# One-hot comparisons for an edge-count matrix: buckets of 512 targets instead of 256, made by two per-part comparisons instead of one interleaved one

## The chip, the cores and the metric

One core of one Trainium2 chip. The metric is device microseconds of one execution of the whole kernel, median of three runs. All times below are of this kernel on this core.

## What is computed

Four graph layers over 6,250 nodes with 96 features and 200,000 edges (`src`, `dst`, sorted by `dst`; low-numbered targets are much more frequent, since `dst` is drawn as 6250·u²):

```
x = x + L0(relu(layernorm(x)))   mean over edges of (h[src] @ W + b)
x = x + L1(relu(layernorm(x)))   gated message MLP with edge_attr_32, sum over edges
x = x + L2(relu(layernorm(x)))   filter MLP of edge_attr_17 times h[src], sum over edges
x = x + L3(relu(layernorm(x)))   three graph convolutions, each a sum over edges and self loops
```

L0 and the three convolutions of L3 need only sums of node rows over edges, so the kernel makes the matrix of edge counts once (`adjacency`: how many edges go from source node s to target node t, 6,272 by 6,272, in f16) and multiplies by it four times.

## The kernel before, in words

The execution has these stretches: edges are loaded and sorted by (block of 128 sources, window of targets) in the block "keys" (to 774 us of the span); the count matrix is made in the block "adjacency" (775 to 1,565 us); L0 multiplies by it; L1 and L2 go over edges; L3 multiplies by the matrix again. The change touches "keys" and "adjacency".

**Buckets and parts.** A bucket is one source block (49 of them) and one window of `WD` = 256 targets (25 of them): 1,225 buckets. The sorted edges are cut into tiles of 128, and a tile that holds several buckets is listed once for each; one such entry is a *part*. Their number is bounded by `PARTS` = 200000 // 128 + 1225 = 2,787, rounded up to 175 turns of `GK` = 16 parts: `T2` = 2,800 parts, all of which are worked off, empty or not.

**A part.** For the 128 edges of a part (one on each partition), VectorE (DVE) writes two one-hot rows in bf16: the source in its block (128 columns) and the target in its window (256 columns). TensorE (PE) multiplies them (`ps_blocks` += sourceᵀ · target), which adds the counts of this part to a panel in PSUM. A panel is a block by 512 targets (two windows), one PSUM bank; there are 8 banks in rotation and 49·13 = 637 panels.

**How DVE makes them before** (L1112 to L1125). One `tensor_tensor` with `is_equal` serves `HK` = 4 parts and all 384 columns: 128x1536 elements, 700 of them. To read lanes of four parts side by side, the innermost dimension is the part, so that the 256 columns of one part lie 4 elements apart, and PE reads them with that stride (`src_hot[:, r, j // HK, :, j % HK]`, L1143). The lane values lie in `lanes` in bf16 (source, target, target minus 128) and are read at an address from a register. Twice a turn DVE loads a register (L1117), waits until PE has used the half of `end_hot` that is to be overwritten (`block_mm`; `end_hot` holds `HB` = 2 turns, 32 parts), and until the bank that the half's last part goes to has been emptied (`emptied`).

**PE** (L1134 to L1145) loads the 16 PSUM columns of a turn from memory into registers and does one 128x256 matmul a part. **ScalarE (ACT)** (L1151 to L1175) waits for a panel's last matmul, copies the bank to `panels` (L1167) and zeroes the bank before it (L1171). **SyncE (SP)** sends each panel to memory (L1200). **GpSimd (POOL)** makes the `heavy_cell` rows (L1184) and sends them (L1190).

**In "keys"**, beside the sort itself, DVE makes one-hot rows of each edge's block and window to count the buckets (`count_chunk`, L763 to L773: 75 instructions in each of 8 chunks); tables of parts are made from 26 scattered writes of POOL (L712) and by `describe_tiles` (L889 to L909) over `T2` elements; the keys of the listed parts are gathered by 24 indirect DMAs of POOL (L718), turned by PE, kept by ACT, and unpacked by DVE (L998 to L1003) to `lanes`, 3,072 elements each.

Order is fixed by the program text: each engine runs its own queue, and semaphores alone join them.

## Time and profile before

| | us |
|---|---|
| three runs | 7378.83, 7361.10, 7363.72 |
| median | 7363.72 |
| span of the profiled execution | 7357.1 |
| of it "keys" and what is ahead of it | 775 |
| of it "adjacency" | 790 |
| of it all after | 5,792 |
| busy over the span: PE / DVE / ACT / POOL | 5543.0 / 4289.6 / 1780.6 / 3246.1 |

The record gives the profiled execution only its span, not a time of its own; the median of the runs is 6.6 us above that span, and the lowest run 4.0 us above it. PE is busy for 75% of the span and DVE for 58%, but these are means over stretches with different limits, so the stretch that the change touches has to be read by itself. Busy time of a matmul includes its latency; the distance between starts in a row of them tells the pace.

### The profile page before, as it was taken

The numbers are of one execution on the slowest core, as the hardware profiler recorded it, in microseconds if no ns is written. First come the engines' busy times: TensorE is split into PE (matmuls) and PEld (weight loads), VectorE is DVE, ScalarE is ACT, GpSimd is POOL, SyncE is SP. The second block draws the span as 40 slices with busy tenths as digits, with TensorE's granted clock in tenths as the row PEclk, the third lists the DMA queues.
The fourth block names the chain that finished last, engine by engine and source line by source line (L and its number), as shares of the span: only waits on it lengthen the run. The fifth ranks groups of instructions, "written<-read, shape, count | busy, mean of one in ns | idle before, by whom it ended". The sixth has DMA issues, their size and how long they took to land. (4 is left out here: it accounts for less than half of the span.)

```text
span 7357.1 us, 136936 instructions
## 1 busy us (share of the span) xinstructions
PE 5543.0 (75%) x29811; PEld 3798.0 (52%) x29813; DVE 4289.6 (58%) x15050; ACT 1780.6 (24%) x3520; POOL 3246.1 (44%) x3354
## 2 busy tenths in 40 slices
PE   3511788869766666666666599999999998899999
PEld 3511344447533433433433366666666666687877
DVE  7887777761278787777777544444444444322222
ACT  0010688850122222222222222222222221100000
POOL 0100500000077777777777177777777775000000
PEclk9975778879888888888888677777777776899999
DMA  1070222236444444444445122222222223466666
GB/s 37 1 237 8 100 100 102 100 126 264 150 93 92 92 92 92 92 92 92 92 92 88 26 47 47 47 47 47 47 47 47 47 47 36 171 262 235 256 241 226
DMA packets 1052581, 764.66 MB, mean 104 GB/s; under 512 B 868977, under 2 KB 978241, under 8 KB 1032914
## 3 DMA queue, kind: packets, MB, share of 16 engines
q1 hardware_dynamic: 664738, 483.03, 21.7%
q0 software_dynamic: 131808, 243.11, 14.1%
q10 hardware_dynamic: 255904, 37.09, 3.0%
q8 instruction: 43, 0.70, 0.0%
q14 instruction: 88, 0.72, 0.0%
HBM read 657.77 MB, written 143.22 MB: 109 GB/s over the span
## 5 line engine op out<-in xcount | busy, mean ns | idle before, releaser
L1869 POOL DMA_INDIRECT rows<-node_rows_wide,idx_ring x1612 | 1537.0, 953 | 501.5 <-issue 426.0
L1869 POOL DMA_INDIRECT rows<-node_rows,idx_ring x1612 | 1522.6, 945 | 492.4 <-issue 491.0
L1918 PE MATMUL ps_sum<-hots,act_ring 128*97 128x128 f32 x3224 | 571.4, 333 | 756.9 <-DVE hots L1903 716.4
L1918 PEld LDWEIGHTS ps_sum<-hots,act_ring 128*97 128x97 f32 x3224 | 463.5, 200 | 1059.2 <-DVE accT L1912 1033.2
L1381 PE MATMUL ps_conv<-conv_rows,adj_ring 128*128 128x288 bf16 x7497 | 941.3, 288 | 45.5 <-DVE conv_rows L1340 21.9
L1912 DVE TENSOR_TENSOR accT<-accT,ps_sum 97x128 f32 (+1 forms) x3224 | 908.8, 282 | 5.0 <-PE ps_sum L1918 4.0
L1381 PEld LDWEIGHTS ps_conv<-conv_rows,adj_ring 128*128 128x128 f16 x7497 | 738.0, 99 | 233.5 <-issue 24.2
L1945 PE MATMUL ps_e<-w1e,aT 128*128 128x384 f32 x1612 | 799.1, 632 | 18.5 <-DVE aT L1981 18.5
L1143 PE MATMUL ps_blocks<-end_hot 128*128 128x256 bf16 x2800 | 673.9, 409 | 112.3 <-DVE end_hot L1123 104.1
L1123 DVE TENSOR_TENSOR end_hot<-iota_h,lanes 128x1536 bf16<-128x1536 bf16 x700 | 631.1, 963 | 156.0 <-ACT ps_blocks L1171 85.0
L2026 PEld LDWEIGHTS ps_w<-w2w,hid 97*128 97x128 f32 x3224 | 478.3, 228 | 469.3 <-issue 390.8
L2046 DVE TENSOR_TENSOR msg<-ps_w,rows 128x384 f32<-128x384 f32 x403 | 224.5, 557 | 785.2 <-DMA rows<-node_rows,idx_ring 728.6
L1918 PE MATMUL ps_sum<-hots,msg 128*96 128x128 f32 x3224 | 608.6, 351 | 90.2 <-DVE hots L1906 74.6
L1906 DVE TENSOR_SCALAR hots<-iota,lane_all 128x128 f32<-128x128 f32 x1612 | 474.4, 297 | 325.6 <-PE ps_sum L1918 250.9
L1989 DVE TENSOR_TENSOR act_ring<-ps_e,rows 128x384 f32<-128x384 f32 x806 | 412.1, 553 | 394.6 <-DMA rows<-node_rows_wide,idx_ring 370.8
L1903 DVE TENSOR_SCALAR hots<-iota,lane_all,gate 128x128 f32<-128x128 f32 x1612 | 587.7, 368 | 14.6
L2026 PE MATMUL ps_w<-w2w,hid 97*128 97x96 f32 x3224 | 550.0, 324 | 60.9 <-DVE msg L2046 44.9
L1918 PEld LDWEIGHTS ps_sum<-hots,msg 128*96 128x96 f32 x3224 | 521.9, 220 | 113.6 <-DVE accT L1912 101.6
L1143 PEld LDWEIGHTS ps_blocks<-end_hot 128*128 128x128 bf16 x2800 | 332.0, 119 | 454.4 <-issue 234.9
L2019 PE MATMUL ps_e<-aT,w 18*96 18x512 f32 x806 | 555.0, 774 | 0.0
L1934 ACT ACTIVATE aT<-ps_t 18x512 f32<-18x512 f32 x403 | 236.2, 586 | 1236.9 <-PE ps_t L1927 1224.1
L1958 ACT ACTIVATE act_ring<-act_ring 128x768 f32<-128x768 f32 x403 | 339.8, 843 | 675.7 <-DVE act_ring L1989 675.7
(341 smaller groups left out, 5879.1 us busy)
## 6 DMA issues: line engine op xcount, KB each, us to landing
adj_ring<-adjacency SPq DMA_DIRECT2D x144, 2176.0 KB, 7.8
adjacency<-panels SPq DMA_DIRECT2D x588, 128.0 KB, 1.7
idx_ring<-sorted_pairs SPq DMA_DIRECT2D x1612, 1.0 KB
attr_ring<-sorted_attr ACTq DMA_DIRECT2D x1612, 16.0 KB
rows<-node_rows_wide,idx_ring POOLq DMA_INDIRECT x1612
attr_ring<-sorted_attr SPq DMA_DIRECT2D x1612, 8.5 KB
rows<-node_rows,idx_ring POOLq DMA_INDIRECT x1612
sorted_attr<-in_edge_attr SPq DMA_DIRECT2D x5, 5000.0 KB
```

Source lines behind the costliest of these rows:

```text
L1123: v.tensor_tensor(end_hot[:, r, n, :, :, :], iota_h[:, :, :].unsqueeze(1).to_broadcast([P, ENDS, P, HK]), lane.to_broadcast([P, ENDS, P, H ...
L1143: pe.matmul(ps_b[:, dyn(at[j], WD)], src_hot[:, r, j // HK, :, j % HK], dst_hot[:, r, j // HK, :, j % HK], start=False, stop=True, skip_gr ...
L1381: last = pe.matmul(ps[:, d, 0:width], ring[:, c, s * cols + d * P:s * cols + (d + 1) * P], nodes[:, c * CB + s, 0:width], start=(c == 0 an ...
L1869: g.indirect_dma_start(out=rows[:, r, j, 0:width], out_offset=None, in_=table, in_offset=bass.IndirectOffsetOnAxis(ap=idx, axis=0)).then_i ...
L1903: last = v.tensor_scalar(hots[:, r % 2, j, :], iota[:, :], lane, gate[:, r % 3, j:j + 1], ALU.is_equal, ALU.mult)
L1906: last = v.tensor_scalar(hots[:, r % 2, j, :], iota[:, :], lane, None, ALU.is_equal)
L1912: v.tensor_tensor(acc, acc, ps_sum[0:M, ra % 2, j, :], ALU.add).then_inc(added.sem, 1)
L1918: last = pe.matmul(ps_sum[0:M, r % 2, j, :], what(r, j), hots[:, r % 2, j, :], start=True, stop=True)
L1945: last = pe.matmul(ps_e[:, r % 2, c, 0:4 * D], aT[:, r % 2, :], w1e[:, 2 * c:2 * c + 2, :].rearrange("p j d -> p (j d)"), start=True, stop ...
L1989: last = v.tensor_tensor(act_ring[:, r % 3, 2 * c:2 * c + 2, :, 0:D].rearrange("p j a d -> p (j a) d"), ps_e[:, r % 2, c, 0:4 * D].rearran ...
L2019: pe.matmul(ps_e[0:D, r % 2, :], w17[:, :], aT[:, r % 2, :], start=True, stop=True).then_inc(edge_mm.sem, 1)
L2026: last = pe.matmul(ps_w[:, r % 2, j, 0:D], hid[:, r % 2, j * P:(j + 1) * P], w2w[:, :], start=True, stop=True)
```

## The change

1. `WD` becomes 512: 13 windows, 637 buckets. `PARTS` = 1562 + 637 = 2,199, so 138 turns and `T2` = 2,208 parts. A window is now a panel and a bank; `NK` = 13 panels a block and their sizes stay as they were, and so does the layout of `adjacency`.
2. DVE makes a part's rows with two `tensor_scalar` instructions, each comparing a row of numbers (`iota_h`, f16) with one value per partition: 128 columns for the source, 512 for the target, written side by side in f16. PE reads them with stride 1.
3. The value per partition is f32, and `lanes` is f32. POOL copies the lanes of four turns (64 parts) at a time into a ring of eight turns (`lane_ring`), so that DVE's addresses are constants. DVE waits for it once in four turns. The loops are unrolled by 8 turns instead of 2.
4. The `heavy_cell` rows are made by DVE in "keys" while the part keys are gathered (26 instructions, L945 of the new text); POOL sends them after its last lane copy.
5. In "keys": 65 instead of 75 instructions a counting chunk, 14 instead of 26 scattered writes, tables of 2,208 instead of 2,800 elements, 20 instead of 24 gathers, and the last unpacking over 2,560 elements in 5 instructions instead of 3,072 in 6.

```
-WD = 256
-ENDS = 1 + WD // P
+QW = 4
+WD = QW * P
+LR = 8
+LH = LR // 2
+HOT = P + WD
...
-            lanes = tmp("lanes", [P, ENDS, TP], BF16)
-            iota_h = tmp("iota_h", [P, P, HK], BF16)
+            lanes = tmp("lanes", [P, 2, TP])
+            iota_h = tmp("iota_h", [P, WD], F16)
+            heavy_cell = tmp("heavy_cell", [P, NK, HV, WD], F16)
...
                     for k in range(NB):
                         v.tensor_scalar(onehots[:, k, :], src_b[:, cols], float(k), None, ALU.is_equal)
-                    v.tensor_copy(onehots[:, NB, :], dst_half[:, cols])
+                    for k in range(1, QW):
+                        v.tensor_scalar(onehots[:, NB + k - 1, :], dst_quarter[:, cols], float(k), None, ALU.is_equal)
                     for k in range(NW):
-                        last = v.tensor_scalar(onehots[:, NB + 1 + k, :], dst_w[:, cols], float(k), None, ALU.is_equal)
+                        last = v.tensor_scalar(onehots[:, LB + k, :], dst_w[:, cols], float(k), None, ALU.is_equal)
...
+                def mark_heavy(v):
+                    for k in range(NK):
+                        cols = PANEL_COLS[k]
+                        for n in range(HV):
+                            last = v.tensor_scalar(heavy_cell[:, k, n, 0:cols], iota_h[:, 0:cols], float(WD * k),
+                                                   heavy_to[:, n:n + 1], ALU.add, ALU.is_equal)
+                    last.then_inc(heavy_cells.sem, 1)
...
                     def hots(q, turn, r):
-                        for n in range(GK // HK):
-                            if n * HK % HALF == 0:
...
-                            lane = lanes[:, :, dyn(q * GK + n * HK, HK)].unsqueeze(2)
-                            v.tensor_tensor(end_hot[:, r, n, :, :, :],
-                                            iota_h[:, :, :].unsqueeze(1).to_broadcast([P, ENDS, P, HK]),
-                                            lane.to_broadcast([P, ENDS, P, HK]), ALU.is_equal).then_inc(ends_hot.sem, 1)
-                    turns(v, [(hots, 0)], Q2, HB)
+                        if r % LH == 0:
+                            v.wait_ge(lanes_in.sem, turn * (LR // LH) + r // LH + 1)
+                        for j in range(GK):
+                            if j % HALF == 0:
...
+                            at = r * GK + j
+                            v.tensor_scalar(end_hot[:, r % HB, j, 0:P], iota_h[:, 0:P], lane_ring[:, 0, at:at + 1],
+                                            None, ALU.is_equal)
+                            last = v.tensor_scalar(end_hot[:, r % HB, j, P:HOT], iota_h[:, :],
+                                                   lane_ring[:, 1, at:at + 1], None, ALU.is_equal)
+                            if j % HK == HK - 1:
+                                last.then_inc(ends_hot.sem, 1)
+                    turns(v, [(hots, 0)], Q2, LR)
...
-                            pe.matmul(ps_b[:, dyn(at[j], WD)], src_hot[:, r, j // HK, :, j % HK],
-                                      dst_hot[:, r, j // HK, :, j % HK],
+                            pe.matmul(ps_b[:, dyn(at[j], WD)], end_hot[:, r % HB, j, 0:P], end_hot[:, r % HB, j, P:HOT],
...
+                    def lane_turns(q, turn, r):
+                        if r % LH == 0:
+                            past(g, ends_hot, (q - LH) * (GK // HK))
+                            g.tensor_copy(lane_ring[:, :, r * GK:(r + LH) * GK],
+                                          lanes[:, :, dyn(q * GK, LH * GK)]).then_inc(lanes_in.sem, 1)
+                    turns(g, [(lane_turns, 0)], Q2, LR)
```

The order of instructions on DVE where the block "adjacency" begins, before. One pair of L1123 rows is half a turn, 8 parts; ISA rows are register work.

```order
L627 UNCONDITIONAL_BRANCH [waits sorted_step]
L1109 UNCONDITIONAL_BRANCH [waits barrier_Pool_Activation_PE_DVE_SP_release]
L1111 MEMSET no_lanes 128x256
L1117 TENSOR_LOAD accT
L1117 ISA x2
L1123 TENSOR_TENSOR end_hot<-iota_h,lanes 128x1536 [waits emptied]
L1123 TENSOR_TENSOR end_hot<-iota_h,lanes 128x1536
```

The same place after the change; the last two rows are one part and come eight times before the next TENSOR_LOAD.

```order
L633 UNCONDITIONAL_BRANCH [waits sorted_step]
L1118 UNCONDITIONAL_BRANCH [waits barrier_Pool_Activation_PE_DVE_SP_release]
L1120 MEMSET no_lanes 128x256
L1128 TENSOR_LOAD accT [waits lanes_in]
L1128 ISA x2
L1134 TENSOR_SCALAR end_hot<-iota_h,lane_ring 128x128 [waits emptied]
L1136 TENSOR_SCALAR end_hot<-iota_h,lane_ring 128x512
```

So where DVE had 2 instructions for 8 parts it has 16, and one new wait (`lanes_in`) in four turns.

POOL in the block "adjacency", before:

```order
L1177 UNCONDITIONAL_BRANCH [waits barrier_Pool_Activation_PE_DVE_SP_gather]
L1179 IOTA target 128x512
L1184 TENSOR_SCALAR heavy_cell<-target,heavy_to 128x512 [waits made]
L1184 TENSOR_SCALAR heavy_cell<-target,heavy_to 128x512 x23
L1184 TENSOR_SCALAR heavy_cell<-target,heavy_to 128x128 x2
L1190 DMA adjacency<-heavy_cell 128x1024 [waits heavy_cells] x12
L1190 DMA adjacency<-heavy_cell 128x2x128 [waits heavy_cells]
L1092 UNCONDITIONAL_BRANCH [waits heavy_out]
```

POOL in the same block after the change; the rows of L152, L162 and ISA are the loop:

```order
L1190 UNCONDITIONAL_BRANCH [waits barrier_Pool_Activation_PE_DVE_SP_gather]
L1196 COPY lane_ring<-lanes 128x2x64 x2
L152 UNCONDITIONAL_BRANCH
L152 ISA
L1196 ISA [waits ends_hot]
L1196 COPY lane_ring<-lanes 128x2x64
L162 REGISTER_ALU
...
L1196 COPY lane_ring<-lanes 128x2x64 [waits ends_hot]
L1202 DMA adjacency<-heavy_cell 128x1024 [waits heavy_cells]
L1202 DMA adjacency<-heavy_cell 128x1024 x11
L1202 DMA adjacency<-heavy_cell 128x2x128
L1104 UNCONDITIONAL_BRANCH [waits heavy_out]
```

The computation of the heavy rows has gone from POOL, 35 short copies have come, and the 13 sends have moved from the first tenth of the block to its end.

## Rows read from the trace of the kernel before

**Rows 1.** Busy time of each engine by stretch, us of the span.
```profile
core 0: us, PE busy (x) PEld busy (x) DVE busy (x) ACT busy (x) POOL busy (x), PEclk, DMA share, GB/s
0.00:776.00 776.00, 226.48 (x1853) 208.45 (x1856) 594.72 (x1225) 43.43 (x65) 69.66 (x73) 0.80 0.21 69
776.00:1565.00 789.00, 675.95 (x2806) 332.50 (x2804) 630.84 (x701) 636.05 (x1273) 79.50 (x40) 0.80 0.31 104
```
**Rows 2.** Costliest groups of 776 to 1565 us: count, busy, mean ns, idle before, releasers.
```profile
L1143 PE MATMUL ps_blocks<-end_hot 128*128 128x256 bf16 x2800 | 673.9, 409 | 112.3 <-DVE end_hot L1123 104.1 <-issue 7.1
L1123 DVE TENSOR_TENSOR end_hot<-iota_h,lanes 128x1536 bf16<-128x1536 bf16 x700 | 631.1, 963 | 156.0 <-ACT ps_blocks L1171 85.0 <-PE ps_blocks L1143 68.7 <-remote 0.7
L1167 ACT ACTIVATE panels<-ps_blocks 128x512 f16<-128x512 f32 x588 | 351.2, 597 | 163.1 <-PE ps_blocks L1143 158.5 <-issue 3.6
```
**Rows 3.** Timeline near 1000 us: start, length, engine, line, count of each merged run.
```profile
999.16 7.18 DVE L1123 TENSOR_TENSOR end_hot<-iota_h,lanes 128x1536 bf16<-128x1536 bf16 x8
1003.44 7.52 PE L1143 MATMUL ps_blocks<-end_hot 128*128 128x256 bf16 x32 [1.08 <-DVE end_hot L1123]
...
1000.56 0.59 ACT L1167 ACTIVATE panels<-ps_blocks 128x512 f16<-128x512 f32 x1
...
1001.55 0.60 ACT L1167 ACTIVATE panels<-ps_blocks 128x512 f16<-128x512 f32 x1
```
**Rows 4.** Stretches of 2 us at the two granted clocks (columns as in rows 1).
```profile
1000.00:1002.00 2.00, 2.00 (x11) 0.92 (x8) 2.00 (x4) 2.00 (x5) 0.00 (x0) 1.00 0.20 70
...
1018.00:1020.00 2.00, 2.00 (x11) 1.05 (x10) 1.96 (x3) 2.00 (x6) 0.00 (x0) 0.50 0.38 131
```
**Rows 5.** Timeline of PE: 512 contiguous columns at 775 us, 289 at 1700 us.
```profile
775.08 3.19 PE L1132 MATMUL ps_blocks<-no_lanes 128*128 128x512 bf16 x7 [14.90 <-DVE no_lanes L1111]
...
1699.77 2.40 PE L1381 MATMUL ps_mean<-mean_rows,adj_ring 128*128 128x289 bf16 x18
```
**Rows 6.** Timeline of DVE: comparisons with a constant, a part of a counting chunk.
```profile
104.99 6.01 DVE L769 TENSOR_SCALAR shared<-lanes 128x196 bf16<-128x196 bf16 x49 [2.50 <-PE ps_counts L1041]
```
**Rows 7.** Timeline of DVE in an edge stage: one value per partition, at a register address.
```profile
5003.15 0.28 DVE L1906 TENSOR_SCALAR hots<-iota,lane_all 128x128 f32<-128x128 f32 x1
5003.35 0.28 DVE L1912 TENSOR_TENSOR accT<-accT,ps_sum 96x128 f32 x1
```
**Rows 8.** DVE groups by shape: no, one and two values per partition at fixed addresses.
```profile
L464 DVE TENSOR_SCALAR blk_i<-accT 128x1568 int32<-128x1568 int32 x1 | 1.0, 977 | 24.8 <-DMA accT<-in_src 24.8
L980 DVE TENSOR_SCALAR keys<-keys,sign 128x2048 f32<-128x2048 f32 x8 | 10.3, 1285 | 0.4
L933 DVE TENSOR_SCALAR keys<-keys,run_f 128x1024 f32<-128x1024 f32 x2 | 1.5, 808 | 0.0
```
**Rows 9.** The first L1123 of the block, and POOL's L1184 and register loads beside it.
```profile
775.33 11.89 DVE L1123 TENSOR_TENSOR end_hot<-iota_h,lanes 128x1536 bf16<-128x1536 bf16 x12 [0.70 <-remote]
...
L1184 POOL TENSOR_SCALAR heavy_cell<-target,heavy_to 128x512 f16<-128x512 f32 x24 | 69.4, 2895 | 1.7
L1184 POOL TENSOR_SCALAR heavy_cell<-target,heavy_to 128x128 f16<-128x128 f32 x2 | 3.4, 1704 | 0.2
L1117 DVEq TENSOR_LOAD <-accT x350: 297/378/866, 774.3 to 1557.1; - x175
```
**Rows 10.** DVE's table work in "keys" over 2800 and 3072 elements, groups by shape.
```profile
L896 DVE TENSOR_TENSOR_SCAN h<-part_bucket,accT 128x2800 f32<-128x2800 f32 x1 | 6.0, 5991 | 0.0
...
L1001 DVE TENSOR_TENSOR lanes<-shared,part_bucket 128x3072 bf16<-128x3072 f32 x1 | 3.4, 3359 | 0.0
L998 DVE TENSOR_SCALAR shared<-keys 128x3072 int32<-128x3072 int32 x1 | 1.8, 1760 | 38.2 <-ACT keys L1089 38.2
```
**Rows 11.** Timeline of POOL: the first and the last of 24 gathers.
```profile
727.77 0.99 POOL L718 DMA_INDIRECT shared<-sorted_keys,part_at  x1 [359.11 <-DMA sorted_keys<-keys]
...
756.54 0.94 POOL L718 DMA_INDIRECT shared<-sorted_keys,part_at  x1 [0.30 <-issue]
```
**Rows 12.** POOL's sends of the heavy rows.
```profile
849.63 7.25 POOL L1190 DMA_DIRECT2D adjacency<-heavy_cell  x13
```

More of the change, by code:

```diff
@@ L101 @@
 CB = SB // NC
-PANEL_COLS = tuple(min(2 * WD, NP - 2 * k * WD) for k in range(NK))
+PANEL_COLS = tuple(min(WD, NP - k * WD) for k in range(NK))
 assert CB * NC == SB and PANEL_COLS[NK - 1] == P
-assert (NB - 1) % BANKS == 0 and TP <= 2 * SN and NK <= 13 and KEYS > E + P and NW <= 1 << WB and COLS % OCN == 0
+assert (Q2 - 1) // LH * LH * GK + LH * GK <= TP and (NB - 1) % BANKS == 0 and TP <= 2 * SN and NK <= 13 and KEYS > E + P and NW <= 1 << WB and COLS % OCN == 0
 ZR = 8
@@ L779, in place_buckets @@
                     v.wait_ge(onehot_used.sem, OCN)
-                    step(v, v.tensor_scalar(of_upper[0:NB + 1, :], of_window[0:NB + 1, :], float(NB), None, ALU.is_equal))
-                    link(v, v.tensor_copy(counts[0:NB + 1, 0:NW], ps_c[0:NB + 1, 0:NW]))
-                    link(v, v.tensor_scalar(of_lower[0:NB + 1, :], of_upper[0:NB + 1, :], -2.0, 1.0, ALU.mult, ALU.add))
+                    for k in range(1, QW):
+                        step(v, v.tensor_scalar(of_quarter[k][0:LB, :], of_window[0:LB, :], float(NB + k - 1), None,
+                                                ALU.is_equal))
+                    step(v, v.tensor_scalar(of_quarter[0][0:LB, :], of_window[0:LB, :], float(NB), -2.0, ALU.is_ge,
+                                            ALU.mult))
+                    link(v, v.tensor_copy(counts[0:LB, 0:NW], ps_c[0:LB, 0:NW]))
+                    link(v, v.tensor_scalar(of_quarter[0][0:LB, :], of_quarter[0][0:LB, :], 1.0, None, ALU.add))
                     v.sem_inc(tables_go.sem, 1)
@@ L833, in place_panels @@
[L833 removed]
+                    link(v, v.tensor_scalar(panel, panel, BANKS - 1, LOG_WD, ALU.bitwise_and, ALU.logical_shift_left))
+                    step(v, v.tensor_copy(panel_f[:, :], panel))
                     link(v, v.tensor_scalar(til[:, :], til[:, :], 1.0, 4096.0, ALU.add, ALU.mult))
[L835 removed]
+                    link(v, v.tensor_tensor(info[:, 0:NW, 2], til[:, :], panel_f[:, :], ALU.add))
@@ L1047, in _ @@
                     pe.wait_ge(tables_go.sem, 1)
-                    pe.matmul(ps_p[:, P:P + NW], of_lower[0:NB + 1, :], counts[0:NB + 1, 0:NW], start=True, stop=True)
-                    pe.matmul(ps_p[:, 2 * P:2 * P + NW], of_upper[0:NB + 1, :], counts[0:NB + 1, 0:NW], start=True,
-                              stop=True).then_inc(tables_in.sem, 1)
+                    for k in range(QW):
+                        last = pe.matmul(ps_p[:, P + k * NW:P + (k + 1) * NW], of_quarter[k][0:LB, :],
+                                         counts[0:LB, 0:NW], start=True, stop=True)
+                    last.then_inc(tables_in.sem, 1)
                     for k in range(2):
@@ L1170, in take @@
                                 a.wait_ge(panel_kept.sem, i * NK + k)
-                                a.activation(ps_b[:, old:old + 2 * WD], none, ACT.Copy).then_inc(emptied.sem, 1)
+                                a.activation(ps_b[:, old:old + WD], none, ACT.Copy).then_inc(emptied.sem, 1)
                     take(0, 0)
```

132 lines of the change are left out of this document (56 added, 76 removed).

## The prediction

> **What bounds the kernel now.** I first read the stretches [rows 1]. The change touches the block "adjacency" (790 us) and some of the 775 us ahead of it; the last 5,792 us keep their instructions and their data layout, so I forecast no difference there. In the block three engines are all 80 to 86% busy, so the second view is its costliest groups [rows 2]: DVE waits 85.0 us for banks that ACT has not yet zeroed and 68.7 us for parts that PE has not yet used; ACT waits 158.5 us for PE, and PE 104.1 us for DVE. Each waits for another by turns. The timeline gives the paces when none waits [rows 3]. DVE: eight comparisons in 7.18 us, so (7.18 - 0.96) / 7 = 0.89 us apart, 0.224 us a part, 2,800 parts make 627 us. PE: (7.52 - 0.41) / 31 = 0.229 us a part, 642 us. ACT: a copy and a zeroing every 0.99 us, 637 panels make about 630 us. Three engines within 3% of each other, joined by short buffers and by panels of very uneven size, take 790 us: about 150 us is their waiting for each other.
>
> PE's pace is not the clock's. At a granted clock of 1.00 (2.4 GHz) and of 0.50 (1.2 GHz) it starts the same 11 matmuls in 2 us [rows 4]. Contiguous columns go faster: 289 of them every (2.40 - 0.287) / 17 = 0.124 us at full clock, 512 every (3.19 - 0.63) / 6 = 0.427 us at the lower one [rows 5]. So before, the stride of four elements binds PE.
>
> **The change, part by part.**
>
> *PE.* 2,208 matmuls of 512 contiguous columns. From [rows 5], 0.124 x 512 / 289 = 0.220 us each at the full clock, 486 us, and 0.427 us, 943 us, if the clock stayed at the lower level throughout. Before, it went back and forth, 0.80 in the mean [rows 1]. PE will move between these two ends.
>
> *ACT and SP.* The same 637 panels, the same bytes: about 630 us, unchanged.
>
> *DVE, the deciding term.* The comparisons lose the interleaving and gain a cheaper element, but they become many. What one costs is a time for its elements and a fixed time. Elements: a `tensor_scalar` on 4-byte data takes (1760 - 977) / (3072 - 1568) = 0.52 ns for each [rows 8, 10]. A comparison of 196 16-bit columns with a constant comes every (6.01 - 0.20) / 48 = 0.121 us [rows 6]. At 0.52 ns its columns would fill 0.102 us and leave 0.019 for everything else; at half, 0.26 ns, 0.051, leaving 0.070, which fits DVE's other pairs. I take 0.26: 0.033 us for 128 columns, 0.133 us for 512. The fixed time: here each instruction reads one value per partition, and the trace has that for f32 data. In [rows 7] L1906, 128 f32 elements at 0.52 ns (0.067 us), is followed 0.20 to 0.21 us later by L1912: 0.138 fixed. That it is the value and not the register address I take from [rows 8], durations at fixed addresses less 0.52 ns an element: 0.160 us without a value (977 - 817), 0.218 with one (1285 - 1067), 0.275 with two (808 - 533). Each value costs some 0.06 us. So a part costs 0.033 + 0.138 + 0.133 + 0.138 = 0.442 us, against 0.224 before, and 2,208 parts make **976 us** against 627. The change saves a fifth of the parts and pays twice for each.
>
> The Trainium skill states otherwise: "VectorE: DVE Perf Modes", section on the TRN2 errata, puts an SBUF-to-SBUF instruction at 58 cycles plus the elements over the mode's factor, with nothing for a value per partition. By that rule a part would be an estimated 0.29 us and DVE's sum about 635 us; rows 7 and 8 are against it, and I take the rows.
>
> *Around them.* Register loads and waits, twice a turn: the loads take 0.378 us on DVE's sequencer [rows 9] beside running work. Before, two comparisons of 0.87 us (1,536 elements at 0.52 ns, 0.80, plus 0.07) took 1.78, so a half turn cost some 0.05 us more; 276 halves, 15 us. Cover is thinner now (instructions of 0.2 us, not 0.9), so up to 0.3 us a half, 80 us, stays as the upper end. POOL's 35 lane copies are asked for four turns ahead, 28 us, so DVE doesn't wait for them, but they share the memory with DVE: while POOL ran L1184, DVE's comparisons came every (11.89 - 0.96) / 11 = 0.99 us, 0.10 more than later, that is 0.3 us for each POOL instruction of 2.9 us [rows 9]. 35 of these are 10 us; if each shut DVE out for 1.7 us, the 128-column L1184, it would be 60. The first copy stands ahead of the first comparison: 2 to 4 us. I take 976 + 15 + 10 + 4 = **1,005 us**.
>
> The page "SBUF — State Buffer" of the Trainium skill, section "SBUF: two separate sides", says that DVE in a two-port mode, or with two inputs in SBUF, and a GpSimd instruction that reads SBUF exclude each other for the whole of an instruction. By it L1184 should have cost the old comparisons far more than the 0.3 us of 2.9 that rows 9 show, and the 35 copies would cost DVE their whole length, an estimated 60 us with L1184's 1.7; I take the rows.
>
> *Waits then.* DVE needs 0.442 us a part, so a block of 45 parts takes 19.9 us, where ACT needs 12.8 and PE at most 19.2. The thinnest full window (targets 5,632 to 6,143) holds 4.2% of a block's 4,082 edges by dst = 6250·u², 172 edges or 2.3 parts, which is 1.04 us of DVE against ACT's 0.99. So the waits for ACT and PE (154 us before) nearly vanish. What is late next is DVE alone.
>
> *POOL's sends.* They took 7.25 us to issue [rows 12] and now start when DVE has six turns, 42 us, to go. Hidden. Were they held up behind DVE, they would add up to 15 us.
>
> *In "keys"* DVE is busy for 77% of the time [rows 1] and is its path. 80 fewer counting comparisons at 0.121 us: -9.7 us, of which PE's counting, for which DVE sometimes waits, takes back perhaps 2. Tables over 2,208 rather than 2,800 elements: three scans of 5.99 us lose 1.27 each, and eight simpler instructions of at least 0.57 ns an element (L998) lose 0.34 each: -6.5. Four gathers fewer, each (756.54 - 727.77) / 23 = 1.25 us apart [rows 11], on which DVE waits 38.2 us [rows 10]: -5. Last unpacking: five of 1.76 us and one of 3.36, now four and one at 5/6 of that: -3.5. The 26 comparisons for the heavy rows, 0.27 us each, 7 us, lie in that same wait of 38 us, of which 33 are left; if it did not cover them they would cost 7. Twelve fewer scattered writes: nothing, as DVE waits for none of them. Sum -23.
>
> **Sum.** 1,005 - 790 = +215, -23, gives +192 us. On the profiled span: 7357.1 + 192 = 7549. The median stands 6.6 us above that span: **7556 us**, +2.6%.
>
> **Rivals.**
>
> *A: DVE doesn't bind, faster.* If the value per partition were fetched behind the instruction ahead, the fixed time would be rows 6's 0.070: 0.307 us a part, 678 + 29 around it = 707 us. ACT's 630 and PE's 486 to 943 stay beside it. Large panels would wait for DVE and small ones for ACT as now; with half of today's 150 us of mutual waiting, 780, less 23: 7,330; with little of it, 730: 7,280. The kernel turns faster from about 0.35 us a part on. For it: two comparisons in a row have no accumulator or PSUM between them as L1906 has. Against: the three durations of rows 8. The skill's fixed 58 cycles, above, would give the same side. 8%.
>
> *B: the f32 value, or f16, denies the faster element.* Then, at 0.52 ns, 0.067 + 0.138 + 0.267 + 0.138 = 0.610 us a part, 1,347 us, and the end is at 7,930. Rows 6 have no value per partition, rows 7 no 16-bit data, so nothing shows the two together. 5%.
>
> *C: the clock makes PE the partner of DVE.* At 0.442 us a part PE works 50% of the time at the full clock and 97% at the lower one. If the lower level holds for most of the block, PE at 0.427, plus what registers and waits add, is as slow as DVE, and two engines of equal pace wait for each other as three do now: 1,070 to 1,110 us, 7,620 to 7,660. For it: the clock falls in the block before too, with PE at 86%. Against: `end_hot` holds 32 parts, which evens out a stretch at the lower clock, and ACT no longer holds either. 12%.
>
> *D: no change that can be measured* (within 0.3%, 22 us; about what a measurement of this kernel can tell from none). It would take a block of 790 to 835 us, 0.35 to 0.37 us a part. No row gives that. 2%.
>
> **The chances.** My forecast 73%: its own range has 0.423 us a part (0.128 fixed, the 0.070 plus 0.058 of rows 8), 934 + 29 us, so 7,514, up to 80 us of loads and 60 of copies on the other side, which will not both come: 7,610. The range takes in the lower part of C: **7,490 to 7,640**. Faster 8%, same 2%, slower 90%.
>
> **What the profile after would show.** Right: L1136 some 0.34 us long and L1134 some 0.24 (0.07 more than they are apart), starts of L1134 0.44 us apart, DVE over 95% busy in the block, block of about 1,005 us; ACT's and PE's waits are for DVE; gathers 20; DVE's wait at the unpacking near 26 us, behind 7 us of heavy rows. Wrong: L1136 of 0.28 us (A) or 0.48 (B); DVE waiting long for PE with a clock near 0.50 (C).

## The result, and the profile after

| | before | after |
|---|---|---|
| median of four runs each, same chip, us | 7366.53 (7361.10 to 7378.83) | 7526.39 (7518.99 to 7530.25) |
| ratio, 95% interval | | 1.0213 (1.0198 to 1.0227) |
| profiled execution: span, us | 7357.1 | 7528.5 |
| "keys" and what is ahead of it | 775.3 | 754.8 |
| block "adjacency" | 789.3 | 972.6 |
| all after | 5,792.5 | 5,801.1 |

The change makes the kernel 2.1% slower. "Keys" gave back 20.5 us, the count matrix took 183 us more. In this document the block runs from DVE's first comparison to its first reduction behind it.

The stretches of the kernel after, to set beside [rows 1]:

```profile
core 0: us, PE busy (x) PEld busy (x) DVE busy (x) ACT busy (x) POOL busy (x), PEclk, DMA share, GB/s
0.00:754.80 754.80, 231.44 (x1852) 214.28 (x1855) 579.82 (x1166) 40.89 (x64) 49.01 (x57) 0.76 0.21 69
754.80:1726.20 971.40, 595.96 (x2212) 218.25 (x2211) 943.25 (x4416) 650.16 (x1273) 19.80 (x46) 0.97 0.25 85
```

Before, three engines were 80 to 86% busy in the block. Now DVE is busy for 97% of it, and PE for 61% at a granted clock of 0.97, where before it was 0.80. The costliest groups in that stretch (busy time and mean of one, then the idle time before them and who ended it) answer to [rows 2]:

```profile
L1136 DVE TENSOR_SCALAR end_hot<-iota_h,lane_ring 128x512 f16<-128x512 f16 x2208 | 761.4, 345 | 0.0
L1157 PE MATMUL ps_blocks<-end_hot 128*128 128x512 f16 x2205 | 593.7, 396 | 375.4 <-DVE end_hot L1136 371.7 <-issue 3.3
L1134 DVE TENSOR_SCALAR end_hot<-iota_h,lane_ring 128x128 f16<-128x128 f16 x2208 | 544.5, 247 | 28.8 <-PE ps_blocks L1157 19.9 <-ACT ps_blocks L1184 7.7 <-remote 0.9
L1184 ACT ACTIVATE ps_blocks<-zeros 128x512 f32<-128x512 f32 x636 | 383.2, 603 | 0.0
L1180 ACT ACTIVATE h<-ps_blocks 128x512 f16<-128x512 f32 x588 | 350.8, 597 | 327.9 <-PE ps_blocks L1157 316.5 <-issue 9.8
```

PE waits 371.7 us for DVE's comparisons and ACT 316.5 us for PE; DVE waits 28.8 us in all, where before it waited 85.0 + 68.7 us. Durations of DVE overlap, so its pace is read from the starts, on the timeline (start, duration):

```profile
1000.14 0.25 DVE L1134 TENSOR_SCALAR end_hot<-iota_h,lane_ring 128x128 f16<-128x128 f16 x1
1000.30 0.34 DVE L1136 TENSOR_SCALAR end_hot<-iota_h,lane_ring 128x512 f16<-128x512 f16 x1
...
1000.57 0.25 DVE L1134 TENSOR_SCALAR end_hot<-iota_h,lane_ring 128x128 f16<-128x128 f16 x1
...
1001.08 1.03 PE L1157 MATMUL ps_blocks<-end_hot 128*128 128x512 f16 x4 [0.96 <-DVE end_hot L1136]
```

The source row is followed 0.16 us later, the window row 0.27 us later. The best ruler for the pace is POOL, which copies the lanes of 64 parts each time DVE is through with 64:

```profile
809.53 0.43 POOL L1196 COPY lane_ring<-lanes 128x128 f32 x1 [26.83 <-DVE end_hot L1136]
836.91 0.43 POOL L1196 COPY lane_ring<-lanes 128x128 f32 x1 [26.94 <-DVE end_hot L1136]
864.17 0.30 POOL L1196 COPY lane_ring<-lanes 128x128 f32 x1 [26.82 <-DVE end_hot L1136]
893.18 0.44 POOL L1196 COPY lane_ring<-lanes 128x128 f32 x1 [28.72 <-DVE end_hot L1136]
```

An undisturbed step is 864.17 - 836.91 = 27.26 us, 0.426 us a part; every other step is some 1.7 us longer (893.18 - 864.17 = 29.01). The cause stands on DVE's own timeline, once every 56 us:

```profile
865.54 0.25 DVE L1134 TENSOR_SCALAR end_hot<-iota_h,lane_ring 128x128 f16<-128x128 f16 x1 [1.55 <-PE ps_blocks L1157]
...
867.56 1.46 PE L1157 MATMUL ps_blocks<-end_hot 128*128 128x512 f16 x3 [2.40 <-DVE end_hot L1136]
...
921.90 0.26 DVE L1134 TENSOR_SCALAR end_hot<-iota_h,lane_ring 128x128 f16<-128x128 f16 x1 [1.62 <-PE ps_blocks L1157]
...
978.02 0.26 DVE L1134 TENSOR_SCALAR end_hot<-iota_h,lane_ring 128x128 f16<-128x128 f16 x1 [1.49 <-PE ps_blocks L1157]
```

56 us are 128 parts, one round of the loop that is unrolled by eight turns. The program text writes out the first round and the last parts and has 16 rounds in the loop between them, so DVE jumps back 15 times. There are 15 pauses of 1.4 to 1.9 us, 23.4 us in all, one at each of these jumps and none where the loop is entered or left. They are most of the 28.8 us; the rest is 2.8 us of waiting for a bank near the end, 0.9 us ahead of the first comparison, and shorter waits. The releaser is given as PE, but PE itself had waited for DVE just before (its four matmuls at 864.13 start after 0.67 us of waiting), so the name is of little use: the pause needed an experiment.

In "keys", the unpacking, to set beside [rows 10], and the heavy rows ahead of it:

```profile
L945 DVE TENSOR_SCALAR heavy_cell<-iota_h,heavy_to 128x512 f16<-128x512 f16 x24 | 6.4, 349 | 0.0
...
L1009 DVE TENSOR_SCALAR shared<-keys 128x2560 int32<-128x2560 int32 x1 | 1.5, 1494 | 28.3 <-ACT keys L1101 28.3
```

### The profile page after: what moved, and what is told of

It reads as the page before. It is cut to its first block and busy times, and to the rows that moved or that the text cites. A ratio compares the mean times of both kernels' runs of the same rounds, so it can differ in the third digit from the quotient of the medians.

```text
span 7528.5 us, 137238 instructions
## 1 busy us (share of the span) xinstructions
PE 5481.1 (73%) x29219; PEld 3697.1 (49%) x29221; DVE 4582.8 (61%) x18707; ACT 1793.5 (24%) x3519; POOL 3174.5 (42%) x3346
## 5 line engine op out<-in xcount | busy, mean ns | idle before, releaser
L1157 PE MATMUL ps_blocks<-end_hot 128*128 128x512 f16 x2208 | 594.4, 396 | 375.4 <-DVE end_hot L1136 371.7
L1136 DVE TENSOR_SCALAR end_hot<-iota_h,lane_ring 128x512 f16<-128x512 f16 x2208 | 761.4, 345 | 0.0
L1157 PEld LDWEIGHTS ps_blocks<-end_hot 128*128 128x128 f16 x2208 | 217.8, 99 | 752.2 <-issue 668.2
L1134 DVE TENSOR_SCALAR end_hot<-iota_h,lane_ring 128x128 f16<-128x128 f16 x2208 | 544.5, 247 | 28.8 <-PE ps_blocks L1157 19.9
```

What stands on the lines that cost most here:

```text
L1134: v.tensor_scalar(end_hot[:, r % HB, j, 0:P], iota_h[:, 0:P], lane_ring[:, 0, at:at + 1], None, ALU.is_equal)
L1136: last = v.tensor_scalar(end_hot[:, r % HB, j, P:HOT], iota_h[:, :], lane_ring[:, 1, at:at + 1], None, ALU.is_equal)
L1157: pe.matmul(ps_b[:, dyn(at[j], WD)], end_hot[:, r % HB, j, 0:P], end_hot[:, r % HB, j, P:HOT], start=False, stop=True, skip_group_check=Tr ...
```

## The experiments

My theory: DVE's fixed cost of a comparison that reads a value per partition makes DVE the only bound. Its rivals as they stood then: another engine or wait, the bucket of 512 itself, the ring, or the long loop. The first four kernels ran on one chip (before: median 7362.48, 7358.30 to 7371.58), the last four too (before: 7359.34, 7354.06 to 7371.39). The four in the middle ran at another time, when every kernel took some 1,400 us longer, the kernel before included (8778.27, 8727.39 to 8810.32); the profiles have this time in the edge stages. Their ratios are to before at that time, so the same number of us makes a smaller ratio there: 1.0215 for "buckets of 512 only" are 196 us, 1.0213 for the change itself 160 us. Of before itself there is no profile from that time; DVE's comparison of 1,536 columns took 964 ns then and 963 at the others.

| kernel | ratio to before, 95% interval | block, us |
|---|---|---|
| constants | 0.9985 (0.9975 to 0.9994) | 804.7 |
| no source row | 0.9948 (0.9932 to 0.9965) | 779.1 |
| loop of 4 turns | 1.0185 (1.0168 to 1.0202) | 948.8 |
| loop of 16 turns | 1.0189 (1.0172 to 1.0206) | 957.0 |
| before, contiguous columns | 0.9995 (0.9976 to 1.0014) | 786.6 |
| before, three turns of buffer | 0.9991 (0.9967 to 1.0016) | 782.6 |
| buckets of 512 only | 1.0215 (1.0174 to 1.0256) | 1008.3 |
| source rows together | 1.0008 (0.9990 to 1.0027) | 816.1 |
| before, one column zeroed | 0.9910 (0.9894 to 0.9925) | 717.0 |
| before, banks zeroed in pairs | 0.9989 (0.9980 to 0.9998) | 789.5 |
| source rows together, pairs | 1.0061 (1.0047 to 1.0075) | 856.1 |
| comparisons only | 1.0353 (1.0337 to 1.0369) | 1045.2 |

### Constants in place of the values

```
-  v.tensor_scalar(end_hot[:, r % HB, j, 0:P], iota_h[:, 0:P], lane_ring[:, 0, at:at + 1],
+  v.tensor_scalar(end_hot[:, r % HB, j, 0:P], iota_h[:, 0:P], float(at % P),
...
-                         lane_ring[:, 1, at:at + 1], None, ALU.is_equal)
+                         float(at), None, ALU.is_equal)
```

> The changed kernel, but both comparisons of a part compare with a constant instead of a value per partition (so the matrix it makes is not the graph's; sizes, waits and number of instructions stay). Theory V (a value per partition costs some 0.06 us an instruction, and DVE's pace sets the block): 0.033 + 0.133 + 2 x 0.070 = 0.306 us a part instead of the 0.426 seen, the 512-column comparison 0.28 us long instead of 0.344; DVE's sum 677 us, near ACT's 640, so the block takes 730 to 790 us instead of 971 and the kernel 7,290 to 7,350. Rival W (the fixed time belongs to any 16-bit comparison side by side, whatever it compares with): nothing changes, above 7,510.

Measured: the time is nearly before's, the block 804.7 us, above the 730 to 790 that were expected. The groups of the block, then the timeline:

```profile
L1136 DVE TENSOR_SCALAR end_hot<-iota_h 128x512 f16<-128x512 f16 x2208 | 624.9, 283 | 3.6 <-issue 3.4
...
L1134 DVE TENSOR_SCALAR end_hot<-iota_h 128x128 f16<-128x128 f16 x2208 | 407.6, 185 | 119.7 <-ACT ps_blocks L1184 104.7 <-PE ps_blocks L1157 9.2 <-issue 4.9
...
L1196 POOL COPY lane_ring<-lanes 128x128 f32 x32 | 69.5, 2171 | 673.4 <-DVE end_hot L1136 673.4
```

```profile
1000.82 0.18 DVE L1134 TENSOR_SCALAR end_hot<-iota_h 128x128 f16<-128x128 f16 x1
1000.92 0.28 DVE L1136 TENSOR_SCALAR end_hot<-iota_h 128x512 f16<-128x512 f16 x1
1001.12 0.18 DVE L1134 TENSOR_SCALAR end_hot<-iota_h 128x128 f16<-128x128 f16 x1
...
1002.34 0.18 DVE L1134 TENSOR_SCALAR end_hot<-iota_h 128x128 f16<-128x128 f16 x1
```

Both comparisons are 62 ns shorter without the value (345 to 283, 247 to 185), and starts of L1134 come 0.304 us apart (1002.34 - 1000.82 over five parts) in place of 0.426. So the value costs DVE 0.06 us each time, 2 x 2,208 x 0.061 = 269 us, and that is what made DVE the bound. But with it gone the block is not 730 to 780 us: DVE is busy 681 us and idle for 123, of which 105 are put down to ACT. Some of these are the loop's: at its 15 jumps back DVE stands 2.1 to 2.6 us each, 34 us in all, mostly with ACT as the releaser. The element rate (0.26 ns in 16-bit data) stands in the same rows: (345 - 247) / 384 = 0.255 ns.

The mean of 2,171 ns for POOL's lane copies hides two kinds. 24 of the 35 copies take 0.28 to 0.31 us. The other 11 take 2.4 to 12.1 us:

```profile
775.41 2.40 POOL L1196 COPY lane_ring<-lanes 128x128 f32 x1 [21.73 <-DVE end_hot L1136]
797.77 0.29 POOL L1196 COPY lane_ring<-lanes 128x128 f32 x1 [19.97 <-DVE end_hot L1136]
821.43 7.27 POOL L1196 COPY lane_ring<-lanes 128x128 f32 x1 [23.36 <-DVE end_hot L1136]
```

These are about one to five times 2.43 us, the time of the eight parts (0.304 us each) that DVE makes between two register loads, and nearly all end where such a run of comparisons ends. A copy that meets such a run is held up to its end, sometimes over several runs.

### No source row

```
-  v.tensor_scalar(end_hot[:, r % HB, j, 0:P], iota_h[:, 0:P], lane_ring[:, 0, at:at + 1],
-                  None, ALU.is_equal)
```

> The changed kernel without the comparison that makes the source rows (they are filled once with ones; the matrix is not the graph's). Theory V (DVE sets the block, 0.163 us for this comparison and 0.263 for the other): 2208 x 0.263 = 581 us, below ACT's 640, so that ACT becomes the bound: block 670 to 740 us, kernel 7,230 to 7,300. Rival P (PE or the waits around it carry a good part of the block): it falls by less than half of the 0.163 x 2208 = 360 us, kernel above 7,350.

Measured: block 779.1 us, where 670 to 740 was expected.

```profile
L1136 DVE TENSOR_SCALAR end_hot<-iota_h,lane_ring 128x512 f16<-128x512 f16 x2208 | 592.8, 347 | 184.5 <-ACT ps_blocks L1184 183.6 <-remote 0.7
...
L1184 ACT ACTIVATE ps_blocks<-zeros 128x512 f32<-128x512 f32 x636 | 386.7, 608 | 0.0
L1180 ACT ACTIVATE h<-ps_blocks 128x512 f16<-128x512 f32 x588 | 351.4, 598 | 155.2 <-PE ps_blocks L1157 144.4 <-issue 10.7
```

With one comparison a part less DVE is busy for only 593 us, and it spends the time that it saves below 780 us in waits for ACT, 184 us. There is a floor near 780 us that DVE does not set. POOL's copies are held up here too, although the comparisons have their values: 16 of the 35 take 2.1 to 6.3 us, about one to three times eight parts of 0.263 us, and 19 take 0.29 to 0.50.

### Loops of four and of sixteen turns

```
-LR = 8
+LR = 4        (the other kernel: LR = 16)
```

> The changed kernel with its loops unrolled by 4 turns instead of 8 (the lane ring holds 4 turns, each copy 2). Theory L (the pause of 1.4 to 1.9 us that DVE makes every 56 us is the jump back of its loop, which comes once in 8 turns): now once in 4 turns, some 33 pauses, one every 28 us, +16 x 1.5 = +25 us, 7,550. Rival M (the pause is a real wait for PE, once in 128 parts, tied to data or buffers): as many pauses as before and 7,515 to 7,535.

> The changed kernel with its loops unrolled by 16 turns. Theory L: 8 pauses instead of 16, one every 112 us, -12 us, 7,514. Rival M: unchanged, 7,520 to 7,535. If a longer loop body pays more at each jump (more to load), the gain is smaller than 12.

Measured: 948.8 and 957.0 us, both below the 972.6 of eight turns. With four turns DVE's waits have shrunk from 28.8 to 6.6 us, and none stands at a jump back. Its busy times in the block, and the instruction queue's packets in the 600 us from 900 us on:

```profile
757.00:1703.00 946.00, 579.18 (x2208) 214.63 (x2205) 938.80 (x4403) 648.97 (x1273) 32.92 (x81) 0.99 0.25 87
```

```profile
q14 instruction: 31, 0.25, 0.2%
```

In the same 600 us of the kernel after (packets, MB, share):

```profile
q14 instruction: 85, 0.70, 0.4%
```

With sixteen turns there is one pause of 1.4 to 2.0 us every 110 us, again one round of the loop (256 parts at 0.426), six in all for six jumps back, and 68 packets. So the pauses come once for each round of a long loop body and go with more fetched instruction data; with four turns there are none. I expected either more of them with the shorter loop or no difference. `LR` also sets the size of the lane ring and of POOL's copies, and unrolls PE's and POOL's loops with DVE's; that these are not the cause is shown by the run with the source rows together, below, which keeps the ring and all loops at eight turns, issues 144 instead of 256 comparisons in a round, and has 38 packets and no such regular pause. The run without the source rows has 128 comparisons in a round of eight turns, 38 packets too, and no regular pause either. That the pause is the time of the fetch itself is the likely reading, not shown.

### Before, with contiguous columns, and with three turns of buffer

```
-  pe.matmul(ps_b[...], src_hot[:, r, j // HK, :, j % HK], dst_hot[:, r, j // HK, :, j % HK], ...
+  pe.matmul(ps_b[...], side_hot[:, r, j // HK, k:k + P], side_hot[:, r, j // HK, k + P:k + P + WD], ...
```

with k = j % HK * (P + WD), and in the other kernel `HB` = 3 in place of 2.

> The kernel before, with one edit: PE reads contiguous columns of the interleaved rows, so the values it multiplies are not the right ones, while every instruction, size and wait stays. Theory S (the stride sets PE's 0.229 us a part, and a third of the 150 us of mutual waiting comes from having PE as a third equal engine): PE falls to 0.11 us a part at full clock and 0.21 at the lower one; DVE 627 and ACT 630 stay; the block takes 700 to 750 us instead of 790, kernel 7,275 to 7,325. Rival T (PE's pace is not from the stride): PE stays at 0.229 and the time at 7,365.

> The kernel before with its ring of one-hot rows one turn deeper (48 parts instead of 32; the panels move to free memory to make room). If the mutual waiting of the three equal engines comes from this ring, DVE's 69 us of waits for PE shrink and the kernel gains 20 to 60 us; if it comes from the 8 banks (DVE's 85 us for ACT), DVE only waits there instead, and the time stays within 15 us of 7,365.

Measured: no difference in time from either. The contiguous columns do what the prediction read from [rows 5]:

```profile
L1122 DVE TENSOR_TENSOR end_hot<-iota_h,lanes 128x1536 bf16<-128x1536 bf16 x700 | 631.2, 964 | 153.5 <-ACT ps_blocks L1170 109.7 <-PE ps_blocks L1142 41.7 <-remote 0.7
L1142 PE MATMUL ps_blocks<-end_hot 128*128 128x256 bf16 x2800 | 505.6, 335 | 277.9 <-DVE end_hot L1122 256.2 <-issue 19.7
```

Back to back, its matmuls start 0.117 us apart at a granted clock of 1.00 and 0.213 at 0.50; before, with the stride, it is 0.230 at both (medians over the block). PE is busy 506 us where it was 674, but the block stays at 786.6, where 700 to 750 was expected: DVE waits less for PE and more for ACT. The stride bound PE, and PE did not bind the block. A third turn of buffer takes it to 782.6, so the waits of 150 us were not for want of buffered parts either.

### Buckets of 512 alone

The buckets and all of "keys" as in the change, but one interleaved instruction serves 4 parts of 640 columns, as before:

```
+  v.tensor_tensor(end_hot[:, r % HB, n, :, :, :],
+                  iota_i[:, :, :].unsqueeze(1).to_broadcast([P, 1 + QW, P, HK]),
+                  lane.to_broadcast([P, 1 + QW, P, HK]), ALU.is_equal)
```

> One part of the change alone: buckets of 512 targets and all that follows in the stage ahead, but the comparisons interleaved by four parts as before (128x2560 bf16) and PE reading with the stride. DVE: (2560 x 0.52 + 97) / 4 = 0.357 us a part, 788 us; PE: twice the strided columns of before, 2 x 0.229 = 0.458, 1,011 us, which now sets the block: 1,020 to 1,080 us, kernel 7,575 to 7,640, slower than the full change. Rival (stride costs PE less in longer rows): DVE sets it, 800 to 850 us, kernel 7,350 to 7,400.

Measured: block 1,008 us, just below the 1,020 to 1,080 that were expected, and longer than the change's.

```profile
L1161 PE MATMUL ps_blocks<-end_hot 128*128 128x512 bf16 x2158 | 990.5, 634 | 14.7 <-issue 11.3 <-DVE end_hot L1141 3.4
L1141 DVE TENSOR_TENSOR end_hot<-accT,lane_mem 128x2560 bf16<-128x2560 bf16 x552 | 783.2, 1486 | 221.3 <-ACT ps_blocks L1188 220.3 <-remote 0.7
```

Eleven strided matmuls take 5.18 us on the timeline, (5.18 - 0.63) / 10 = 0.455 us each, twice the 0.229 of 256 columns. 2,208 of them are 1,004 us: here PE binds, and DVE's wait named ACT is PE's, one link further on (ACT waits 364 us for PE). So wide buckets need contiguous columns, and the change could not have had the one without the other.

### Comparisons alone

Windows of 256 as before, 2,800 parts, two comparisons a part and the ring as in the change; the rows of the heavy cells are left out and filled with zeros.

```
 v.tensor_scalar(end_hot[:, r % HB, j, 0:P], iota_h[:, 0:P], lane_ring[:, 0, at:at + 1], ...
 v.tensor_scalar(end_hot[:, r % HB, j, P:HOT], iota_h[:, :], lane_ring[:, 1, at:at + 1], ...
-QW = 4
+WD = 256
```

> One part of the change alone: windows stay 256 targets wide (2,800 parts of comparisons, two windows to a bank as before), but the source and window rows are two comparisons side by side against a value per partition, and the lane values come through the ring. The rows of the heavy cells are replaced by zeros, so some counts are left out. My theory, that the fixed cost of a comparison with a value per partition is 0.130 us and the element costs 0.26 ns: 2,800 x (0.130 + 0.033 + 0.130 + 0.067) = 1,008 us, plus some 22 pauses of 1.5 us, one for each round of the loop, and a few us at the start: block 1,020 to 1,060 us, whole kernel 2.8 to 3.8% slower than before. So the side-by-side comparisons lose by themselves some 230 to 270 us of the block, and the wide bucket (fewer parts) gives 50 to 80 us back. Rival: the columns side by side let TensorE and the comparisons run denser and win some of it, block under 980 us.

Measured: block 1045.2 us, ratio 1.0353, as the fixed cost wants it.

```profile
L1129 DVE TENSOR_SCALAR end_hot<-iota_h,lane_ring 128x256 f16<-128x256 f16 x2800 | 768.2, 274 | 0.0
...
L1127 DVE TENSOR_SCALAR end_hot<-iota_h,lane_ring 128x128 f16<-128x128 f16 x2800 | 680.2, 243 | 37.6 <-ACT ps_blocks L1178 17.5 <-PE ps_blocks L1150 13.2 <-issue 6.2
```

DVE's busy time in the stretch is 1,006.8 us against 1,008 forecast, and 37.6 us are waits and pauses. There are 19 pauses of 1.8 to 2.3 us for 19 jumps back. They are 48 us apart, 128 parts at 0.36 us and the pause itself, so they keep to the loop's round and not to a time of their own; and their releaser changes from one to the next, among them "issue", which is nothing that the profile shows:

```profile
921.45 0.25 DVE L1127 TENSOR_SCALAR end_hot<-iota_h,lane_ring 128x128 f16<-128x128 f16 x1 [1.80 <-issue]
969.57 0.25 DVE L1127 TENSOR_SCALAR end_hot<-iota_h,lane_ring 128x128 f16<-128x128 f16 x1 [2.09 <-issue]
```

PE works at a granted clock of 0.52 in this block, where the change's had 0.97, and still waits 345 us for DVE, so the lower clock is not what makes this block long. The comparisons by themselves cost 1045.2 - 789.3 = 256 us of the block, and the wide bucket gives 1045.2 - 972.6 = 73 us back.

### Source rows of eight parts together

The change, with the source rows of 8 parts made by one interleaved instruction, and window rows as in the change:

```
+  if j % SK == 0:
+      v.tensor_tensor(src_hot[:, r % HB, j // SK, :, :], iota_s[:, :, :],
+                      src_lanes[:, dyn(q * GK + j, SK)].unsqueeze(1).to_broadcast([P, P, SK]), ALU.is_equal)
```

> The changed kernel, but the source rows of 8 parts are made by one interleaved comparison of two tensors (128x1024 bf16), the target rows as in the change. DVE: (1024 x 0.52 + 90) / 8 = 0.078 us for the source rows, 0.263 for the target rows, 0.341 a part, 753 us, plus 24 us of pauses; PE keeps contiguous moving columns. Block 780 to 820 us instead of 971, kernel 7,335 to 7,380, about level with the kernel before. If the weights with a stride of 8 elements slow PE, or if ACT with 640 us takes part in the waiting, it is at the upper end or beyond.

Measured: block 816.1 us, the whole kernel equal to before.

```profile
1001.32 2.19 DVE L1143 TENSOR_SCALAR end_hot<-iota_h,lane_ring 128x512 f16<-128x512 f16 x8
1003.42 0.68 DVE L1140 TENSOR_TENSOR src_hot<-accT,lanes 128x1024 bf16<-128x1024 bf16 x1
1004.02 2.18 DVE L1143 TENSOR_SCALAR end_hot<-iota_h,lane_ring 128x512 f16<-128x512 f16 x8
```

Eight parts take 1004.02 - 1001.32 = 2.70 us, 0.338 us each: nearly half of the fixed costs are gone, with 156.5 of the 183 us that the block had lost. At 0.338 us a part the two kernels are level.

### Before, with one column of a bank zeroed

```
-  a.activation(ps_b[:, old:old + 2 * WD], none, ACT.Copy)
+  a.activation(ps_b[:, old:old + 1], none[:, 0:1], ACT.Copy)
```

> The kernel before, but ScalarE zeroes one column of a finished PSUM bank instead of all 512: a piece of work left out to read its price, and later blocks count on top of what stands in the banks. Theory F: the 783 to 805 us at which the block stands in every kernel without the costlier comparison (before, the constants, the left-out source row, the contiguous columns, the deeper ring) is ScalarE's chain of some 637 panels at about 1.0 us, 400 ns of it the zeroing, with 145 to 165 us of waiting for the first large panel of each block of sources. With the zeroing at 170 to 200 ns ScalarE is busy about 450 to 510 us, and the block becomes shorter by some 70 to 110 us, to 680 to 720 us; VectorE, busy 620 us, is then the next engine. Whole kernel 1.0 to 1.5% faster than before. Rival G: the block is set by the three engines waiting for each other in turn through the two buffers; VectorE's waits for ScalarE then turn into waits for TensorE, and the block stays at 770 to 785 us, the time within 0.3% of before.

Measured: block 717.0 us, 0.9% off the whole.

```profile
L1123 DVE TENSOR_TENSOR end_hot<-iota_h,lanes 128x1536 bf16<-128x1536 bf16 x700 | 624.7, 964 | 89.8 <-ACT ps_blocks L1171 60.1 <-PE ps_blocks L1143 28.6 <-PE ps_blocks L1132 0.7
...
L1171 ACT ACTIVATE ps_blocks<-zeros 128x1 f32<-128x1 f32 x636 | 113.2, 178 | 0.0
```

This is the only edit of before that moved its block by more than 7 us: what ACT does with the banks is behind the floor. Its busy time fell from 636 to 377 us and the block by 72, within the 680 to 720 us that theory F expected. The edit shortens ACT's work and gives each bank back sooner, both at once.

### Banks zeroed in pairs

ACT zeroes 1,024 columns after every second panel; once in before, with three turns of buffer, and once in the kernel with the source rows together, there with a loop of four turns.

```
-  if k > 0 or later:
+  if (place * NK + k) % 2 == 0 and (k > 0 or later):
-      a.activation(ps_b[:, old:old + WD], none, ACT.Copy).then_inc(emptied.sem, 1)
+      a.activation(ps_b[:, old - WD:old + WD], none, ACT.Copy).then_inc(emptied.sem, 2)
```

> The kernel before with a third turn of buffer, and ScalarE zeroing two finished banks (1,024 columns) by one instruction after every second panel instead of one bank after each. Theory F: a zeroing of 1,024 columns takes some 750 to 800 ns against two of 400 ns, so 0 to 50 ns less for each of about 318 pairs, and its sequence costs are paid once: 10 to 25 us of ScalarE's 636 us, and the block is 755 to 775 us: whole kernel 0.1 to 0.4% faster than before. Against it: a bank is given back one panel later, and TensorE may wait for it where a block of sources begins; then VectorE's and TensorE's waits grow and the time stays within 0.1% of before or lies above it. Rival G expects no change.

> The change with the source rows of 8 parts built together by one instruction (as in the run with the sources together, whose block took 815 us), a loop of four turns, and ScalarE zeroing two banks by one instruction. VectorE: 2,208 window rows and 276 instructions of 687 ns for the source rows, about 750 us as measured there; ScalarE 610 to 625 us. Theory F: the 63 us of waiting for ScalarE fall by 10 to 25 us, block 790 to 805 us, whole kernel within 0.2% of before, to either side. If the later return of banks costs, it stays at 815 us or more.

Measured: the block missed what was expected in both. In before ACT's busy time in the block fell to 615 us, and the block stayed at 789.5, 7 us above the run with three turns alone:

```profile
L1123 DVE TENSOR_TENSOR end_hot<-iota_h,lanes 128x1536 bf16<-128x1536 bf16 x700 | 631.3, 963 | 156.1 <-ACT ps_blocks L1171 97.4 <-PE ps_blocks L1143 53.0 <-PE ps_blocks L1132 0.7
```

In the other kernel it grew from 816.1 to 856.1, DVE's waits for ACT from 63 to 101 us with its busy time unchanged (751 and 753):

```profile
L1140 DVE TENSOR_TENSOR src_hot<-accT,lanes 128x1024 bf16<-128x1024 bf16 x276 | 189.0, 685 | 102.2 <-ACT ps_blocks L1191 101.1 <-PE ps_blocks L1153 0.8
```

So it isn't ACT's busy time alone that counts. That it is how soon a bank comes back, so that fewer and later hand-backs cost at least what the shorter work gains, fits both runs, but no run changes the one without the other. The ratio of 0.9989 in before doesn't come from the block, and is about what a measurement can tell from no change. No version that keeps all the work beats before by more than that. Two forms of the change are better than it: the loop of four turns is 24 us shorter in the block, and the one with the source rows together is level with before.

## Why the prediction was right

Direction, size and mechanism held: 7,556 us forecast, 7,526 measured, inside the range. Of the 29 us between them, 32 are the block (+215 us forecast, +183 measured) and 9 the step from span to median, less 2.5 from "keys" and 8.6 from the later stages. The median was put 6.6 us above the profiled span, as before; it came out 2.1 us below it, since the profiled execution was the slowest of the four.

**The deciding term: right, 4% too large.** 0.442 us a part were forecast, 0.426 measured. The elements are as taken (0.255 ns against 0.26); the fixed cost is (0.426 - 0.166) / 2 = 0.130 us, not the 0.138 of L1906 [rows 7]. It is close to the "0.070 plus 0.058" that the prediction kept for the lower end of its range, and the constants show both parts of it: (0.304 - 0.166) / 2 = 0.069 without the value, 0.061 for the value. 2,208 x 0.426 = 941 us, not 976. The steps that were right are those that took the price of a value per partition from [rows 8], 0.058 us for one, and the element from [rows 6]. [Rows 8] compare instructions of different lengths and types (int32 and f32), so they were no proof; the run with constants, which changes nothing but the value, is. One slip has no weight: 0.89 us for four parts of before are 0.222 us each, 622 us in all, not 0.224 and 627.

The Trainium skill's page "VectorE: DVE Perf Modes", section on the TRN2 errata, has 58 cycles and the elements over the mode's factor. The comparisons with constants agree with it nearly (0.304 us a part against the estimated 0.29); those with a value (0.426) do not, and the formula has no term that tells the two apart.

**Around them: forecast 29 us, found near none of it, and 29 us of another kind.** Registers and waits (15 us) don't show: starts of L1134 are 0.425 us apart within a half turn and across its border alike (medians). Where a POOL copy falls a part takes some 0.03 us more, 1 us for all 35, not 10. Ahead of the first comparison DVE waits 0.93 us, where before it waited 0.70; 4 were forecast for the first copy. What the prediction had not at all is the pause at each jump back of the loop, 28.8 us with the rest of DVE's waits. 941 + 29 + 3 = 973; of the last 3, 1.5 lie between the last comparison and the reduction, and the rest isn't assigned. That the two sums of 29 agree is luck.

**"Keys": -20.5 against -23.** The wait at the unpacking fell from 38.2 to 28.3 us (26 forecast, behind 7 us of heavy rows, which took 6.8), and each pass of the unpacking from 1.76 to 1.49 us. The 20 gathers are 1.25 us apart as forecast, but the first took 3.1 us in place of 0.99, which is about the missing 2 us. The heavy sends (1681 to 1688 us) lie before the block's end at 1727, hidden.

**The later stages** were forecast with no difference and took 8.6 us more in the profiled execution. In the other kernels of the first and the last four, and in before, they took 5,785 to 5,797 us, so most of it is within what profiles differ by; nothing in the runs assigns it.

**Rival A** (the value hidden) fell: L1136 is 345 ns, not 280. Its price was wrong too. It put a block without the value at 730 to 780 us and the time at 7,280 to 7,330; the constants are exactly that case, at 0.304 us a part where A had 0.307, and the block took 804.7, the whole 7,353. The step that failed is "half of today's 150 us of mutual waiting". The three engines of [rows 2] looked alike, but they are not: edits of DVE, PE and buffer left the floor of 779 to 805 us, an edit of ACT's zeroing took 72 us off it. The 34 us of pauses at the loop's jumps had no term in A either; whether they are why this block is the longest of those on the floor is not shown. **B** fell with the first row: 0.255 ns an element. **C** fell too: the clock stayed at 0.97, and the 20 us that DVE is said to have waited for PE are for the most part the loop's pauses. **D** stood on a block of 790 to 835 us from 0.35 to 0.37 us a part. The kernel with the source rows together has such a block, 816.1, and is level with before, but at 0.338 us.

## What to carry to other kernels

Before replacing one wide interleaved instruction by several narrow ones, multiply their number by the fixed cost, and take that cost from an instruction with the same kinds of operands: a value per partition doubled it here, and 4,416 times 0.13 us outweighed a fifth fewer parts and an element at half the price. Engines that are equally busy are not equally binding: shorten each one's work in a run of its own before counting on slack. After unrolling a loop, look for a pause at the loop's period. And look at single instructions before believing a mean: POOL's copies of 2.17 us are 0.29 us or whole runs of comparisons.

## What the runs showed of the hardware

- A VectorE comparison with a value per partition has a fixed 0.130 us between starts, with a constant 0.069 (f16 data, 128 and 512 columns).
- A matmul whose columns lie four elements apart takes 0.229 us for 256 columns at either granted clock, and 0.455 for 512 at 1.00; contiguous ones come four in 1.03 us, (1.03 - 0.38) / 3 = 0.217 us apart for 512 at 1.00, and 0.117 us (1.00) or 0.213 us (0.50) apart for 256.
- VectorE pauses once at each jump back of a loop with 256 comparisons in its body (1.4 to 1.9 us in the change, 1.8 to 2.3 with comparisons alone) or with 512 (1.4 to 2.0 us), and not with 128 or 144, nor where the loop is entered or left.
- POOL's lane copy takes 0.29 to 0.55 us in the change, and delays DVE by some 0.03 us. With constants 11 of 35 copies take 2.4 to 12.1 us, and with the window rows alone, which have values, 16 of 35 take 2.1 to 6.3 us; the others take 0.28 to 0.50. What decides between the two is not shown. The Trainium skill's page "SBUF — State Buffer", section "SBUF: two separate sides", says that a VectorE instruction in a two-port mode, or with two inputs in SBUF, and a GpSimd one that reads SBUF hold each other out for a whole instruction. The long copies agree in that POOL is held out, but for up to 79 comparisons and not for one of 0.28 us; the copies in the change show no such wait.
